# A mixture-of-experts tail with its second layer transposed and its combine weights spread over partitions by a transfer

## The chip, the cores and the metric

One core of one Trainium2 chip (trn2). The metric is the device time of one execution in microseconds (us), median of several; lower is better.

## What is computed

Two transformer layers on x of B = 2 batches, S = 512 tokens, D = 128 features, all in fp32. The parts of the last stage are what the change touches:

```python
# after two attentions: x = layernorm(x + attn_out)
gp = softmax(xt @ w_group + b_group); g_idx = argmax(gp); g_prob = max(gp)
ep_sel = softmax(xt @ w_expert[g_idx] + b_expert[g_idx]); e_idx = argmax(ep_sel); e_prob = max(ep_sel)
combine = one_hot(g_idx * 2 + e_idx, 8) * (g_prob * e_prob)          # (tokens, 8)
h = relu(einsum('td,edf->etf', xt, w1) + b1)                          # 8 experts, 256 hidden
y = einsum('etf,efd->etd', h, w2) + b2
out = layernorm(xt + einsum('te,etd->td', combine, y)) + x1           # x1 is the layer's input
```

Ahead of it stand a ternary-weight FFN with 8-bit activations and two 16-head attentions (the first one causal, with an image key). Every expert is computed for every token.

## The kernel before, in words

The kernel is written engine by engine with semaphores. `MERGE` (line 46) is a string in which each letter takes the next step of one chain of work, and `program_order()` (line 58) turns it into one list of steps. Every engine walks the same list and issues its part of each step, in that order, so the string alone sets the order on all queues: TensorE (PE), VectorE (DVE), ScalarE (ACT), GpSimd (POOL) and SyncE (SP, whose queue issues nearly all DMAs). Steps are named with an instance: 0 and 1 are the two batches in the first attention, 2 and 3 in the second; in the expert stage 0 and 1 are the batches. Below, y1.3 is step `y` of batch 1, expert 3.

PSUM is cut into places: `misc`, `pv`, `s0`, `s1` of one bank (512 fp32 columns) and `t0`, `t1` of two. `place_jobs()` (line 137) counts the jobs of each place in the order of the list; PE waits before it writes a place until all earlier jobs of that place have been freed, and readers wait for the fill count.

The order of the stages: the FFN of batch 0 (steps ffn_in to x1t), the small products `images` (PE lines 1156 to 1174, for which DVE and ACT take the results at lines 905 and 719), q, k and v of batch 0, three-part bf16 splits of q and k on DVE (lines 950 to 963), which SP writes to DRAM and loads back stacked (line 501), then the `scores` of all instances (PE line 1253, row maxima on DVE lines 985 and 989), beside them `attend` (PE line 1276, exp on ACT line 770) and `values` (PE line 1294). Scores of batch 0 wait for the stacked q and k.

The expert stage, per batch, with the lines of each step:

- `presum` and `sum` (PE lines 1321 to 1331) form x + attention in rows, `centre` and `spread` normalise it on DVE (lines 817 to 833) with a power on POOL (line 639), `x3t` transposes it into X3T (PE line 1337, ACT line 776).
- `router` (PE line 1345), `routed` and `route` (DVE lines 1038 to 1075) give `comb`, a column of 8 weights for each token; `combine` transposes it to combT, 8 partitions of 512 tokens (PE line 1352, ACT line 779); `bias2` multiplies it with b2 (four matmuls, PE line 1359) and `acc0` adds X3 into acc (DVE line 1080).
- For each of the 8 experts `hidden` makes two 128x512 halves of the first layer in s0 and s1 (PE line 1369, two matmuls of 512 columns), `relu` is taken on DVE for s0 (line 1084) and on ACT for s1 (line 756) into `hid`, which has two buffers; `y` (PE line 1377) uses `hid` as the weights and W2 as the streamed operand, in 4 token tiles by 2 halves, 8 matmuls of 128 columns, into `misc`; `add` (DVE line 1093) adds each of the 4 tiles, times the token's combine weight, to acc.
- At the end `centre` and `spread` with i = 1 normalise acc and add x1, and SP stores it (line 550).

A 4-byte matmul shows as two MATMUL records, so `y` is 16 records and `hidden` is 4. The expert steps of batch 0 start while the attention of instance 3 is still running; those after it follow on PE almost back to back.

## Time and profile before

| | |
|---|---|
| median of 3 runs | 357.32 us (356.76 to 358.71) |
| the profiled execution's own time | 352.93 us |
| its span | 351.1 us |
| busy: PE, PE weight loads, DVE, ACT, POOL | 293.8, 149.9, 258.8, 168.8, 29.3 us |
| mean granted TensorE clock | 0.96 |
| DMA | 22.83 MB |

The span is the time from the first to the last instruction of the profile; the execution's own time has 1.8 us more around it. Busy times overlap. A matmul's end is modelled, so distances between starts are the better measure on PE. A row of the views below says engine, line, output<-input, shape and count, then busy time, mean, and what ended the idle time before.

### The profile page before, as it was taken

Reading aid. Unit: us, or ns where it says so; the run is one execution under the profiler, and the core shown is the slowest. Engines: PE = TensorE matmul, PEld = TensorE weight load, DVE = VectorE, ACT = ScalarE, POOL = GpSimd, SP = SyncE. Lnnn points to the kernel's source line nnn. Section 1 sums busy time; section 2 is a strip of 40 time slices with the busy share of each in tenths; the row PEclk is TensorE's granted clock in tenths of the full one; section 3 lists DMA queues with packets and bytes.
Section 4 is the critical chain, followed back from the end, with each engine's and each line's share of the span. In section 5 each row is a group of like instructions: output and inputs, shape, how many; then the busy total and the mean of one; then the engine's idle time right before and its main releaser. Section 6 shows DMA issues by size and latency. Waiting matters only on the chain.

```text
span 351.1 us, 5408 instructions
## 1 busy us (share of the span) xinstructions
PE 293.8 (84%) x1862; PEld 149.9 (43%) x1888; DVE 258.8 (74%) x764; ACT 168.8 (48%) x246; POOL 29.3 (8%) x58
## 2 busy tenths in 40 slices
PE   0286945988889999789999999999899999899981
PEld 0134531345445554244342332334334457656760
DVE  6888687999767788979999788777813128558445
ACT  1864360055555686166286676674767621221110
POOL 3075000000000000600000000003000001001001
PEclk9999686599999999999999999999999999999997
DMA  6892157214620027800037500260000000001001
GB/s 191 177 194 57 27 158 175 58 34 141 166 57 3 2 74 200 156 7 2 2 86 189 130 1 0 56 187 2 0 2 2 0 2 1 2 0 30 0 2 31
DMA packets 14959, 22.83 MB, mean 65 GB/s; under 512 B 2190, under 2 KB 12306, under 8 KB 14164
## 3 DMA queue, kind: packets, MB, share of 16 engines
q1 hardware_dynamic: 14644, 22.21, 25.7%
q0 software_dynamic: 288, 0.28, 0.7%
q8 instruction: 15, 0.25, 0.3%
q14 instruction: 12, 0.10, 0.1%
HBM read 13.99 MB, written 4.72 MB: 53 GB/s over the span
## 4 chain that ended last, share of the span: by engine, by line
PE 43%; DVE 22%; issue 14%; DMA 10%; ACT 6%; SPq 2%; POOL 1%; POOLq 0%; another core or an unknown queue 0%; DVEq 0%; ACTq 0%
PE ps_pv L1294 10%; DVE mx L989 9%; PE ps_t L1276 7%; PE ps_s L1253 6%; DMA Qs<-nmT 6%; PE ps_s L1369 5%; PE ps_misc L1377 4%; ACT probs L770 3%; DVE shared L985 2%; DMA shared<-in_L_ffn_w_down 2%; DVE probs L919 1%; DVE shared L833 1%; DVE q L922 1%; DVE mx L985 1%; DMA Ks<-parts_k 1%
## 5 line engine op out<-in xcount | busy, mean ns | idle before, releaser
L770 ACT ACTIVATE probs<-ps_t 128x1024 f32<-128x1024 f32 (+2 forms) x128 | 105.6, 862 | 61.8 <-PE ps_t L1279 26.4
L989 DVE TENSOR_REDUCE mx<-ps_s 128x1 f32<-128x512 f32 x126 | 80.8, 685 | 13.7 <-PE ps_s L1253 12.4
L1253 PE MATMUL ps_s<-Ks,Qs 128*128 128x512 bf16 (+3 forms) x220 | 70.6, 347 | 11.0 <-DVE mx L985 2.8
L1276 PE MATMUL ps_t<-Qs,Ks 128*128 128x512 bf16 (+3 forms) x245 | 65.4, 338 | 6.2 <-DMA Qs<-nmT 3.8
L1294 PE MATMUL ps_pv<-probs,Vs 128*32 128x512 f32 (+3 forms) x512 | 55.5, 522 | 0.3 <-ACT probs L770 0.2
L985 DVE CUSTOM_DVE_ANT_0 shared<-ps_s,shared 128x128 bf16<-128x128 f32 (+3 forms) x106 | 45.6, 459 | 10.4 <-PE ps_s L1253 9.5
L1253 PEld LDWEIGHTS ps_s<-Ks,Qs 128*128 128x128 bf16 x232 | 21.7, 98 | 57.9 <-DVE mx L989 26.8
L1093 DVE SCALAR_TENSOR_TENSOR shared<-ps_misc,comb,shared 128x128 f32<-128x128 f32 x64 | 18.0, 343 | 31.1 <-PE ps_misc L1377 31.1
L1276 PEld LDWEIGHTS ps_t<-Qs,Ks 128*128 128x128 bf16 x256 | 23.5, 98 | 32.4 <-issue 10.7
L1377 PE MATMUL ps_misc<-Ks,shared 128*128 128x128 f32 x256 | 31.6, 277 | 4.2 <-DVE shared L1093 1.4
L1377 PEld LDWEIGHTS ps_misc<-Ks,shared 128*128 128x128 f32 x256 | 30.5, 192 | 9.6 <-issue 8.2
L1369 PE MATMUL ps_s<-Qf,Ks 128*128 128x512 f32 x64 | 30.3, 596 | 0.0
L756 ACT ACTIVATE shared<-ps_s,cols 128x512 f32<-128x512 f32 x16 | 11.0, 686 | 36.7 <-PE ps_s L1369 36.7
L1279 PE MATMUL ps_t<-causal_k,identb 128*128 128x128 bf16 x128 | 24.5, 219 | 0.3 <-issue 0.2
L1294 PEld LDWEIGHTS ps_pv<-probs,Vs 128*32 128x32 f32 x512 | 11.4, 108 | 21.2 <-issue 20.0
L639 POOL TENSOR_TENSOR shared<-shared,halves 128x4 f32<-128x4 f32 x4 | 4.1, 1036 | 193.7 <-DVE shared L823 193.7
L753 ACT ACTIVATE shared<-ps_pv 128x512 f32<-128x512 f32 x16 | 9.6, 597 | 12.1 <-PE ps_pv L1294 12.0
L1369 PEld LDWEIGHTS ps_s<-Qf,Ks 128*128 128x128 f32 x64 | 11.0, 191 | 9.5 <-issue 9.0
L1084 DVE TENSOR_SCALAR shared<-ps_s,cols 128x512 f32<-128x512 f32 x16 | 11.9, 744 | 3.4 <-PE ps_s L1369 3.4
L1279 PEld LDWEIGHTS ps_t<-causal_k,identb 128*128 128x128 bf16 x128 | 12.5, 98 | 3.2 <-issue 0.3
L985 DVE CUSTOM_DVE_ANT_0 shared<-ps_t,shared 128x512 bf16<-128x512 f32 (+1 forms) x22 | 13.0, 626 | 0.0
L633 POOL TENSOR_TENSOR Zimg<-Vimg,Pimg 128x288 f32<-128x288 f32 x4 | 2.7, 682 | 107.6 <-ACT Pimg L750 107.6
(244 smaller groups left out, 324.2 us busy)
## 6 DMA issues: line engine op xcount, KB each, us to landing
parts_q<-Qp SPq DMA_DIRECT2D x20, 128.0 KB, 1.9
Qs<-parts_q SPq DMA_DIRECT2D x24, 96.0 KB
Ks<-parts_k SPq DMA_DIRECT2D x24, 96.0 KB
Qs<-parts_q SPq DMA_DIRECT2D x12, 192.0 KB
Ks<-parts_k SPq DMA_DIRECT2D x12, 192.0 KB
Ks<-Qs SPq DMA_DIRECT2D x2, 1024.0 KB, 12.0
parts_k<-Kp SPq DMA_DIRECT2D x12, 128.0 KB, 1.8
Qs<-Qs SPq DMA_DIRECT2D x1, 1024.0 KB, 12.2
```

The lines of the kernel that those rows point to most:

```text
L756: act.activation(hid[:, i % 2, 1, :], ps[:, :], ACT.Relu, bias=cols17[:, 2 * i + 1:2 * i + 2])\
L770: act.activation(probs[:, half % 2, j, 0:w], ps[:, 0:w], ACT.Exp).then_inc(free[f"t{i % 2}"], 1)
L985: last = dve.tensor_tensor_reduce(out=added[:, n % 2, 0:w], in0=ps[:, 0:w], in1=causal_q[:, S - w:], scale=1.0, scalar=LEAST, op0=ALU.add, ...
L989: last = dve.tensor_reduce(mx[:, b, t, h:h + 1], ps[:, 0:w], AX, ALU.max)
L1084: dve.tensor_scalar(hid[:, i % 2, 0, :], ps[:, :], cols17[:, 2 * i:2 * i + 1], 0.0, ALU.add, ALU.max).then_inc(free["s0"], 1)
L1093: last = dve.scalar_tensor_tensor(out=acc[:, a, t, :], in0=ps[:, t * D:(t + 1) * D], scalar=comb[:, a, t, i // 2, i % 2:i % 2 + 1], in1=ac ...
L1253: mm = pe.matmul(ps[:, 0:w], Qs[:, b, h, t * P:(t + 1) * P], Ks[:, b, h, 0:w], start=True, stop=True)
L1276: mm = pe.matmul(ps[:, col:col + w], Ks[:, b, h, kb * P:(kb + 1) * P], Qs[:, b, h, S - w:S], start=True, stop=(a >= 2))
L1279: mm = pe.matmul(ps[:, col:col + P], identb[:, :], causal_k[:, :], start=False, stop=True)
L1294: mm = pe.matmul(ps[j * HC:(j + 1) * HC, S - w:S], Vs[:, b, kb, r * GROUP + j, :], probs[:, half % 2, j, col:col + w], start=(kb == 0), st ...
L1369: pe.matmul(ps[:, :], W1[:, i, h * P:(h + 1) * P], X3T[:, a, :], start=True, stop=True)\
L1377: mm = pe.matmul(ps[:, t * D:(t + 1) * D], hid[:, i % 2, h, t * P:(t + 1) * P], W2[:, i, h, :], start=(h == 0), stop=(h == FH - 1))
```

## The change

1. `y` takes W2 as weights and streams `hid`: two matmuls of 512 columns, out transposed (features on partitions, tokens along the row). For batch 0 each expert's result goes to `misc` and DVE adds it to accT; for batch 1 all 16 matmuls and `bias2` accumulate in `pv`, and DVE adds once, in two halves.
2. The combine weight now multiplies `hid` (new step `scale`, two 128x512 products on DVE for each expert). The weights must stand along the row on all 128 partitions: SP writes combT (16 KB) to DRAM, waits for it, and loads it back to combB with every partition reading the same rows, 512 KB for experts 0 and 1 and 1.5 MB for the other six, each with its own semaphore. combB lies in Qs.
3. `relu` of both halves is on ACT.
4. `bias2` is one matmul of 512 columns.
5. A new step `rows` turns accT back (4 transposes), and `centre` reads that from PSUM.
6. `MERGE` is another string, with other places for steps of every stage. Among them: `images` stands after k0 instead of ahead of the third `ffn_up` of batch 1; `x1` of batch 1 on DVE stands after 5 steps of scores instead of before the first; POOL's `stacks` of batch 0 stands ahead of `turn_weights`; `load_small` is earlier and `load_experts` 5 scores later.

The order of PE's steps in the last stage, before:

```
y0.1 values hidden0.2 turn_back hidden0.3 o_rows presum1 y0.2 sum1 hidden0.4 y0.3 hidden0.5 y0.4 hidden0.6
x3t1 y0.5 hidden0.7 router1 y0.6 hidden1.0 combine1 y0.7 hidden1.1 bias2_1 y1.0 hidden1.2 y1.1 hidden1.3 y1.2
hidden1.4 y1.3 hidden1.5 y1.4 hidden1.6 y1.5 hidden1.7 y1.6 y1.7
```

and after:

```
y0.1 values hidden0.2 turn_back hidden0.3 o_rows presum1 y0.2 sum1 hidden0.4 y0.3 hidden0.5 x3t1 y0.4
hidden0.6 y0.5 hidden0.7 router1 y0.6 combine1 hidden1.0 bias2_1 y0.7 hidden1.1 rows0 y1.0 hidden1.2 y1.1
hidden1.3 y1.2 hidden1.4 y1.3 hidden1.5 y1.4 hidden1.6 y1.5 hidden1.7 y1.6 y1.7 rows1
```

The diff, cut to its core:

```diff
+        accT = XT
+        combB = Qs[:, :, :, :].rearrange("p b h s -> p b (h s)").bitcast(fp32)\
+            .rearrange("p b (e s) -> p b e s", e=EXPERTS)
...
+                if step == "combine":
+
+                    sp.wait_ge(free["misc"], filled("misc", "combine", a))
+                    sp.dma_start(comb_dram[a], combT[:, a, :]).then_inc(comb_stored[a], 16)
+                    sp.wait_ge(comb_stored[a], 16)
+                    sp.wait_ge(full["t1"], filled("t1", "weights", 2 + a, UNITS - 1))
+                    for g, (lo, hi) in enumerate(((0, 2), (2, EXPERTS))):
+                        sp.dma_start(combB[:, a, lo:hi, :].rearrange("p e s -> p (e s)"),
+                                     drows(comb_dram[a][lo:hi, :], P, (hi - lo) * S)).then_inc(comb_spread[a][g], 16)
...
                 if step == "relu":
-                    ps = take("s1", "hidden", a, i)
-                    act.activation(hid[:, i % 2, 1, :], ps[:, :], ACT.Relu, bias=cols17[:, 2 * i + 1:2 * i + 2])\
-                       .then_inc(free["s1"], 1)
+                    for h in range(FH):
+                        ps = take(f"s{h}", "hidden", a, i)
+                        act.activation(hid[:, i % 2, h, :], ps[:, :], ACT.Relu,
+                                       bias=cols17[:, 2 * i + h:2 * i + h + 1]).then_inc(free[f"s{h}"], 1)
...
+                    dve.wait_ge(free["misc"], filled("misc", "x3t", a))
+                    dve.tensor_tensor(accT[:, a, :], ps[:, :], X3T[:, a, :], ALU.add).then_inc(free["misc"], 1)
+                if step == "scale":
+                    dve.wait_ge(comb_spread[a][i // 2 > 0], 16)
+                    for h in range(FH):
+                        dve.wait_ge(free[f"s{h}"], filled(f"s{h}", "hidden", a, i))
+                        last = dve.tensor_tensor(hid[:, i % 2, h, :], hid[:, i % 2, h, :], combB[:, a, i, :], ALU.mult)
+                    last.then_inc(scaled, 1)
+                if step == "add" and a == 0:
...
-                    for t in range(NT):
-                        last = dve.scalar_tensor_tensor(
-                            out=acc[:, a, t, :], in0=ps[:, t * D:(t + 1) * D],
-                            scalar=comb[:, a, t, i // 2, i % 2:i % 2 + 1], in1=acc[:, a, t, :],
-                            op0=ALU.mult, op1=ALU.add)
-                    last.then_inc(free["misc"], 1)
+                    dve.tensor_tensor(accT[:, a, :], ps[:, :], accT[:, a, :], ALU.add).then_inc(free["misc"], 1)
+                if step == "add" and a == 1:
+                    ps = take("pv", "outputs", a)
+                    dve.wait_ge(free["misc"], filled("misc", "x3t", a))
+                    half = S // 2
+                    for n in range(2):
+                        last = dve.tensor_tensor(accT[:, a, n * half:(n + 1) * half], ps[:, n * half:(n + 1) * half],
+                                                 X3T[:, a, n * half:(n + 1) * half], ALU.add).then_inc(summed[a], 1)
...
+                    ps = put("misc", "bias2", a) if a == 0 else put("pv", "outputs", a)
+                    mm = pe.matmul(ps[:, :], B2[:, :], combT[:, a, :], start=True, stop=(a == 0))
...
                 if step == "y":
+                    pe.wait_ge(scaled, NTH["scale", a, i])
+                    ps = put("misc", "y", a, i) if a == 0 else place["pv"]
                     for h in range(FH):
+                        mm = pe.matmul(ps[:, :], W2[:, i, h, :], hid[:, i % 2, h, :],
+                                       start=(a == 0 and h == 0), stop=(h == FH - 1 and (a == 0 or i == EXPERTS - 1)))
...
+                if step == "rows":
+                    if a == 0:
+                        pe.wait_ge(free["misc"], filled("misc", "y", a, EXPERTS - 1))
+                    ps = put("misc", "rows", a)
                     for t in range(NT):
-                        for h in range(FH):
-                            mm = pe.matmul(ps[:, t * D:(t + 1) * D], hid[:, i % 2, h, t * P:(t + 1) * P],
-                                           W2[:, i, h, :], start=(h == 0), stop=(h == FH - 1))
+                        if a == 1:
+                            pe.wait_ge(summed[a], t // 2 + 1)
+                        mm = pe.transpose(ps[:, t * P:(t + 1) * P], accT[:, a, t * P:(t + 1) * P], ident[:, :])
                     mm.then_inc(full["misc"], 1)
```

## Rows read from the trace of the kernel before

**Rows 1.** Windows of 20 us: busy time of PE, PEld, DVE, ACT, POOL; clock, DMA, GB/s
```profile
60.00:80.00 20.00, 17.30 (x75) 8.01 (x74) 19.48 (x89) 5.89 (x9) 0.68 (x1) 0.74 0.22 53
...
300.00:320.00 20.00, 17.18 (x104) 12.39 (x102) 11.79 (x49) 3.95 (x7) 1.04 (x1) 1.00 0.00 1
```

**Rows 2.** Groups by line and shape, 280 us to the end
```profile
L1377 PE MATMUL ps_misc<-Ks,shared 128*128 128x128 f32 x224 | 27.7, 277 | 4.2 <-DVE shared L1093 1.4 <-DVE shared L1080 0.9 <-ACT Qf L776 0.8
L1377 PEld LDWEIGHTS ps_misc<-Ks,shared 128*128 128x128 f32 x224 | 26.6, 192 | 9.3 <-issue 8.2 <-DVE shared L1084 1.0
...
L1093 DVE SCALAR_TENSOR_TENSOR shared<-ps_misc,comb,shared 128x128 f32<-128x128 f32 x57 | 16.1, 343 | 22.8 <-PE ps_misc L1377 22.8
```

**Rows 3.** The chain that ended last: start us, length us, what
```profile
290.99 1.72 PE ps_s L1369 x4
292.70 1.78 PE ps_misc L1377 x16
...
300.00 0.45 PE ps_misc L1337 x4
...
304.96 0.81 PE ps_misc L1345 x8
...
314.83 1.10 PE ps_misc L1359 x8
```

**Rows 4.** PE's waits from 290 us on: total us, times, longest
```profile
PE ps_misc L1377 <- DVE shared L1093: 1.4, 1, 1.4
PE ps_misc L1377 <- DVE shared L1080: 0.9, 1, 0.9
PE ps_misc L1377 <- ACT Qf L776: 0.8, 1, 0.8
```

**Rows 5.** Groups by line and shape, whole span
```profile
L770 ACT ACTIVATE probs<-ps_t 128x1024 f32<-128x1024 f32 x64 | 62.5, 1021 | 27.1 <-PE ps_t L1276 24.0 <-remote 1.7 <-PE ps_pv L1294 1.1
...
L756 ACT ACTIVATE shared<-ps_s,cols 128x512 f32<-128x512 f32 x16 | 11.0, 686 | 36.7 <-PE ps_s L1369 36.7
...
L1080 DVE TENSOR_TENSOR shared<-ps_misc,shared 128x512 f32<-128x512 f32 x2 | 1.4, 690 | 8.4 <-PE ps_misc L1359 8.4
```

**Rows 6.** Timeline of the expert stage: start us, length us, engine, line
```profile
308.33 0.18 DVE L1074 TENSOR_TENSOR comb<-rg,comb 128x16 f32<-128x16 f32 x1
...
341.21 2.02 PE L1377 MATMUL ps_misc<-Ks,shared 128*128 128x128 f32 x16 [1.38 <-DVE shared L1093]
343.34 1.12 DVE L1093 SCALAR_TENSOR_TENSOR shared<-ps_misc,comb,shared 128x128 f32<-128x128 f32 x4 [2.28 <-PE ps_misc L1377]
```

**Rows 7.** DMA issues: out<-in, count, KB each, median us from issue to landing
```profile
parts_q<-Qp SPq DMA_DIRECT2D x20, 128.0 KB, 1.9
...
Ks<-Qs SPq DMA_DIRECT2D x2, 1024.0 KB, 12.0
...
Ks<-in_L_ffn_w SPq DMA_DIRECT2D x1, 1024.0 KB, 5.8
```

**Rows 8.** A 2 us window while the two 1 MB expert weights load
```profile
229.00:231.00 2.00, 2.00 (x14) 0.57 (x13) 1.68 (x3) 1.48 (x2) 0.00 (x0) 1.00 1.08 344
```

**Rows 9.** Timeline from the small products to the first scores
```profile
34.42 0.38 PE L1159 MATMUL ps_s<-WsqT,condT 128*128 128x128 f32 x2
...
35.23 1.12 DVE L946 SCALAR_TENSOR_TENSOR X<-ps_pv,q,X 128x128 f32<-128x128 f32 x4
...
38.12 1.63 PE L1173 MATMUL ps_s<-WinT,WcpT 128*128 128x384 f32 x2
...
45.60 0.69 DVE L953 TENSOR_TENSOR qres<-Qf,Qp 128x512 f32<-128x512 f32 x1
...
49.18 0.75 DVE L936 TENSOR_SCALAR shared<-probs 128x512 bf16<-128x512 f32 x2
...
55.66 0.33 PE L1253 MATMUL ps_s<-Ks,Qs 128*128 128x128 bf16 x2 [2.13 <-issue]
```

**Rows 10.** The window in which exp, the first experts and the last attention overlap
```profile
248.00:278.00 30.00, 29.02 (x181) 13.18 (x185) 9.99 (x35) 22.30 (x28) 0.00 (x0) 1.00 0.00 1
```

More of the change, by code:

```diff
@@ L98, in program_order @@
         "y": both("y", EXPERTS),
-        "z": both("add", EXPERTS),
+        "z": each("add", 0, EXPERTS) + [("add", 1, EXPERTS - 1)],
+        "&": both("scale", EXPERTS),
     }
@@ L110, in program_order @@
         chains["ns"[b]] = [(n, b, 0) for n in ("presum", "sum", "x3t", "router", "combine", "bias2")]
-        chains["QR"[b]] = [(n, b, 0) for n in ("centre", "spread", "routed", "route", "acc0")]
-        chains["op"[b]] = [("centre", b, 1), ("spread", b, 1), ("out", b, 0)]
+        chains["QR"[b]] = [(n, b, 0) for n in ("centre", "spread", "routed", "route")] + [("acc0", 0, 0)] * (b == 0)
+        chains["op"[b]] = [("rows", b, 0), ("centre", b, 1), ("spread", b, 1), ("out", b, 0)]
     taken = {name: iter(steps) for name, steps in chains.items()}
@@ L164, in place_jobs @@
         if step in ("x1t", "q", "k", "v", "o_rows",
-                    "x3t", "router", "combine", "bias2"):
+                    "x3t", "router", "combine", "rows") or step == "bias2" and a == 0:
             add("misc", step, a)
+        if step == "bias2" and a == 1:
+            add("pv", "outputs", a)
         if step == "presum":
@@ L187, in place_jobs @@
             waiting -= 1
-            add("misc", "y", a, i)
+            if a == 0:
+                add("misc", "y", a, i)
     return places
@@ L233, in two_layers @@
                        for n, count in (("q", 2 * PARTS - 1), ("k", PARTS))] for a in range(INST)]
+        comb_dram = [nc.dram_tensor(f"parts_comb{b}", (EXPERTS, S), fp32, kind="Internal").ap() for b in range(B)]
         ident = sb("ident", [P, P])
@@ L428, in two_layers @@
         rstd_ready = [sem(f"rstd_ready{n}") for n in range(2 * B)]
-        gained = [sem(f"gained{b}") for b in range(B)]
         x3_ready = [sem(f"x3_ready{b}") for b in range(B)]
@@ L432, in two_layers @@
         comb_ready = sem("comb_ready")
+        comb_stored = [sem(f"comb_stored{b}") for b in range(B)]
+        comb_spread = [[sem(f"comb_spread{b}_{g}") for g in range(2)] for b in range(B)]
+        scaled, summed = sem("scaled"), [sem(f"summed{b}") for b in range(B)]
         out_ready, stored = [sem(f"out_ready{b}") for b in range(B)], sem("stored")
@@ L1079, in _ @@
                     ps = take("misc", "bias2", a)
-                    dve.tensor_tensor(acc[:, a, :, :], ps[:, :].rearrange("p (t d) -> p t d", d=D),
-                                      X3[:, a, :, :], ALU.add).then_inc(free["misc"], 1)
-                if step == "relu":
-                    ps = take("s0", "hidden", a, i)
-                    dve.tensor_scalar(hid[:, i % 2, 0, :], ps[:, :], cols17[:, 2 * i:2 * i + 1], 0.0,
-                                      ALU.add, ALU.max).then_inc(free["s0"], 1)
-                if step == "add":
+                    dve.wait_ge(free["misc"], filled("misc", "x3t", a))
[7 more added lines that the diff above has]
+                if step == "add" and a == 0:
                     if i == 0:
@@ L1091, in _ @@
                     ps = take("misc", "y", a, i)
[L1092 to L1097 removed]
+                    dve.tensor_tensor(accT[:, a, :], ps[:, :], accT[:, a, :], ALU.add).then_inc(free["misc"], 1)
[6 more added lines that the diff above has]
+                                                 X3T[:, a, n * half:(n + 1) * half], ALU.add).then_inc(summed[a], 1)
                 if step == "centre" and i == 1:
[L1099 to L1100 removed]
+                    ps = take("misc", "rows", a)[:, :].rearrange("p (t d) -> p t d", d=D)
+                    centre(2 + a, ps, acc[:, a, :, :], 2).then_inc(free["misc"], 1)
                 if step == "spread" and i == 1:
[L1102 removed]
+                    dve.wait_ge(free["misc"], filled("misc", "rows", a))
                     dve.wait_ge(residual_ready[a], 1)
@@ L1356, in _ @@
                     pe.wait_ge(free["misc"], filled("misc", "combine", a))
-                    ps = put("misc", "bias2", a)
-                    for t in range(NT):
-                        mm = pe.matmul(ps[:, t * D:(t + 1) * D], combT[:, a, t * P:(t + 1) * P], B2[:, :],
-                                       start=True, stop=True)
-                    mm.then_inc(full["misc"], 1)
+                    ps = put("misc", "bias2", a) if a == 0 else put("pv", "outputs", a)
+                    mm = pe.matmul(ps[:, :], B2[:, :], combT[:, a, :], start=True, stop=(a == 0))
+                    if a == 0:
+                        mm.then_inc(full["misc"], 1)
                 if step == "hidden":
```

26 lines of the change are left out of this document (13 added, 13 removed).

## The prediction, made before the change was run

> **What bounds the kernel now.** I read the windows first. From 60 to 80 us DVE is the full engine, with 19.48 of 20 us busy; from 300 to 320 us it is PE, with 17.18 of 20 against 11.79 for DVE and 3.95 for ACT [rows 1]. The change rewrites the expert stage, so its price is read on PE. The groups by shape say that y's matmuls are spaced by the work and not by waits: 4.2 us of waiting against 27.7 us busy in 14 steps [rows 2]. The chain gives the distances: two hidden matmuls of 512 columns take 1.72 us, and a y step of eight of 128 columns takes 1.78 us [rows 3]. Both stream 1024 columns. The waits name what stops PE there, each time because `misc` is still held: 1.4 us for the last adds, 0.9 us for acc0, 0.8 us for the copy of X3T [rows 4].
>
> **y.** The new y streams 2 times 512 columns, the shape of hidden, so I take 1.72 for 1.78 us: 0.06 us for each of 16, 1.0 us in all. The twelve weight loads that go were under the matmuls already. They are 26.6 us of busy time in 14 steps, 1.9 us a step [rows 2]; beside matmuls of 1.71 us nose to tail they would make a step 3.6 us long, and it is 1.78 us.
>
> The Trainium skill ("TensorE: Matmul & The Clock Gate", "The mechanism") says that a weight load overlaps a running matmul only when the row group differs. These all use the whole array, so by that rule the loads lie on the path and the change saves far more. By it the sum would be that of rival 5, by the trace it is the 1.0 us above. The trace disagrees with the rule, with its 1.78 us.
>
> **DVE and ACT.** The four adds of 343 ns [rows 2] and DVE's half of relu go; two products of 128x512 come, at 690 ns like acc0 [rows 5], 1.38 us, and for batch 0 one add of 0.69 us. ACT takes two relus of 686 ns [rows 5], 1.37 us. PE needs 3.44 us for a hidden and a y, so both are hidden wherever PE has a full pair to do. They would show where y follows its hidden closely. The last one does: hidden1.7 ends, y1.6 runs 1.72 us, then y1.7 needs relu and product, 0.7 + 0.7 us. 0.3 us of cover are left.
>
> **The expert stage on PE.** Let S be the end of sum1 (290.99) and R the end of router1 (305.77) [rows 3]. Before, R is S+14.8.
> - S to R holds the same steps. x3t1 is earlier, and the copy of X3T stands behind relu0.5 on ACT, so y0.4 waits 1.0 us where y0.5 waited 0.8 [rows 4]; three y and their restarts give some 0.6 back. R is S+14.4.
> - Before, after R: y0.6, hidden1.0, combine1, y0.7, hidden1.1, bias2, y1.0 and on, with PE's end at 341.21+2.02 = 343.23 [rows 6], R+37.5.
> - After: y0.6 waits 0.4 us for `routed` and ends at R+2.2. Now combine1 is next. It needs comb, which stood at 308.33+0.18 [rows 6], R+2.75, and `misc`, which add0.6 frees; that add is behind route on DVE, so R+3.45. PE idles 1.3 us. This is new: hidden1.0 covered that stretch. combine1 ends at R+4.0 and its copy on ACT, priced like a relu of 0.69 us [rows 5], at R+4.7.
> - PE goes on: hidden1.0 R+5.7, bias2 (0.9 us as one matmul, 1.10 as four [rows 3]) R+6.6, y0.7 R+8.3, hidden1.1 R+10.0, rows0 (0.45 like x3t [rows 3]) R+10.5. y1.0 could start there.
> - The spread: SP writes 16 KB, which lands after 1.9 us like the writes of parts_q [rows 7], and issues the loads at R+6.7. The 512 KB lie between 1.9 us for 128 KB and 5.8 us for 1 MB [rows 7], so 3.4 us, landing at R+10.1; the products end at R+11.5. y1.0 waits 1.0 us.
> - The other 1.5 MB: the expert weights move at 344 GB/s [rows 8], so 2 MB take 6.1 us and about 2 us of start and landing: R+15. By the row of 5.8 us for 1 MB it would be R+17. y1.2 would start at 11.5+4x1.72 = R+18.4 and needs it by R+17.0. No wait, with little or no margin at the dear end.
> - From y1.0 there are 14 pieces of 1.72 us: PE ends at R+35.6 instead of R+37.5. The waits of 0.9 and 1.4 us are gone, since y of batch 1 no longer shares `misc`.
>
> Sum: y0.0 to y0.2 -0.2, S to R -0.4, after R -1.9: -2.5 us.
>
> **The end.** Before, the last adds take 1.12 us after PE [rows 6]. Now two half adds of some 0.4 us (a 512-column one is 0.69 [rows 5]), with the first transposes under the second, then the last two transposes and their way out, 1.3 us. +0.2 us. centre and spread keep their price, as does the store.
>
> **The spread of batch 0.** The same sum as above gives 1.9+3.4+1.4 = 6.7 us and some issue time from the copy of combine0 to the end of the products. Between combine0 and y0.0 stand ten attend steps, whose exps of 1.02 us each [rows 5] alone are 10.2 us. So it is hidden. Without that cover PE would wait at y0.0 for what is late, with attention queued behind it, and exp on ACT after that.
>
> **relu on ACT beside exp.** From 248 to 278 us ACT is busy 22.3 of 30 us and PE 29.0 [rows 10]. Two more relus of 0.69 us come in. Free if they fall in ACT's gaps, 1.4 us if PE waits for each. I take 0.5, since PE is the fuller engine.
>
> **The new order.** `images` leaves the path of batch 0. It holds PE from 34.42 to 39.75 [rows 9] while x1t0 could start at 36.35, when the sums of x1 are done [rows 9]. With it gone DVE does ffn_up1.2 and 1.3 from 37.7 us and starts the parts of q near 41.6 instead of 45.60 [rows 9], 4 us earlier; so k's parts and both loads. But `images` then stands between k0 and batch 1's r2t on PE (41.8 to 47.3) and its copy is ahead of r2t's work on ACT, so DVE reaches r2t1.0 at 48.6 instead of 49.18 [rows 9]. The down products end near 53, and scores start there instead of at 55.66 [rows 9]: -2.6 us. x1 of batch 1, 1.12 us [rows 9], now falls into the full DVE stretch and was in the gap before it. Net -1.5 us, which I carry to the end, since DVE and then PE are full in between. Bounds: 0 (lost at a later join) and -4 (q's lead all used). Moves of single values, turns and sends by a few steps in the middle have no price that I can read: none, between -2 and +2.
>
> **POOL and SP.** POOL's earlier memsets fall into a wait. load_small goes onto POOL's queue, load_experts onto SP's, both far ahead of need. SP's wait for the stored 16 KB has only `out` behind it; no max_rows step follows combine.
>
> **Sum.** -2.5 + 0.2 + 0.5 - 1.5 = -3.3 us on an execution of 352.93 us: 349.6. That execution is 4.4 us under the median of the runs shown, so I move the median by as much: 357.3 - 3.3 = 354.0 us.
>
> **Rivals.**
> 1. *The spread arrives late (slower).* Every partition reads the same 16 KB of DRAM, which no transfer here does at this size. Against it: 344 GB/s [rows 8] with rows shorter than these. For it: a 1 MB copy from 64 partitions to 64 others took 12.0 us [rows 7]. It decides once the 1.5 MB land after R+17.0, 10.3 us after the issue; each us beyond is one on PE. At 12 us a MB they land at R+31, and 512 KB at R+13: y1.2 starts at R+32.3 instead of 18.4, +14 us, 368 us. At 160 GB/s they take 14 us, +4 us, no gain: 358 us.
> 2. *The order's gain is lost.* The first stage's 1.5 us go at a later join, and relu beside exp costs its 1.4: -2.5+0.2+1.4 = -0.9, 356.4 us. For it: ACT and PE are both near full in [rows 10].
> 3. *The order costs.* The middle loses 2 to 4 us at the long waits for the row of maxima behind the stacks: 357 to 360 us.
> 4. *q's lead is used in full.* -4 instead of -1.5: 351.5 us.
> 5. *Weight loads are on the path.* Then 12 of 16 loads of each y, 1.4 us, go: 16x1.4 = 23 us, 331 us. The 1.78 us of [rows 3] speak against it. (The rule of the Trainium skill quoted above would give this.)
>
> That the change doesn't do what it says: the stream of columns is the same, so the transposition itself gives 1 us. It is in the forecast.
>
> **How the numbers follow.** A measurement of this kernel can tell about 0.5%, 1.8 us, from no change. Forecast (352.3 to 355.5) 42%, rival 4 13%, rival 5 1%; rival 2 23%; rival 3 9%, rival 1 12%, of which a third ends within 1.8 us. Faster: 42+13+1 = 56%. Same: rival 2, part of 1 and 3, 27%. Slower: 17%. The range reaches down over rival 4 with -2 us of the middle, 349.5, and up over rival 3, 360.
>
> **What would show it.** y as 4 records in 1.72 us; first scores near 53 us; PE idle 1.3 us ahead of combine1 and 1.0 us ahead of y1.0; no wait of PE for `misc` in batch 1; scale1.2 not waiting for the transfer beyond R+17; PE's end at S+50. Wrong if y is much shorter than 1.72 us, if DVE waits for combB for more than a us or two, or if the first scores start at 55 us or later.

## The result and the profile after

| | before | after |
|---|---|---|
| median of 20 runs each | 356.64 us (352.44 to 361.86) | 360.96 us (355.31 to 370.22) |
| the profiled execution's span | 351.1 us | 355.5 us |
| busy: PE, PE weight loads, DVE, ACT | 293.8, 149.9, 258.8, 168.8 us | 293.7, 131.2, 256.3, 180.7 us |

The change makes the kernel slower: ratio after to before 1.0156, 95% interval [1.0108, 1.0205]. (Ratios leave disturbed, slower runs out and medians here are of all runs, so the two can differ by up to 0.8 per cent; where they disagree, neither is taken to settle a step smaller than that.) The forecast was 354.0 us; the time also lies above its range, which ended at 360.

**The expert stage is what I said.** Two parts of the chain of after, start us, length us, what:

```profile
297.11 1.72 PE ps_s L1393 x4
298.83 1.72 PE ps_misc L1399 x4
...
310.73 0.81 PE ps_misc L1370 x8
...
314.19 0.69 DVE XT L1115
314.88 0.14 issue
315.02 0.61 PE ps_misc L1377 x4
315.65 0.59 ACT X L800
316.26 1.45 DMA parts_comb<-X
317.73 4.08 DMA Qs<-parts_comb
```

A y step is 4 records in 1.72 us instead of 16 in 1.78 [rows 3]. S, the end of sum1, is 297.11 here and 290.99 before. R, the end of router1, is 311.54: S+14.4, as worked out. PE's waits from 296 us on:

```profile
PE ps_misc L1377 <- DVE XT L1115: 1.2, 1, 1.2
PE ps_misc L1399 <- ACT Qf L797: 0.9, 1, 0.9
PE ps_pv L1399 <- DVE shared L1107: 0.7, 1, 0.7
```

1.2 us ahead of combine1 (1.3 forecast) and 0.7 us ahead of y1.0, which waits for the spread weights (1.0 forecast). The row of y1.0:

```profile
323.19 1.98 PE L1399 MATMUL ps_pv<-shared,Ks 128*128 128x512 f32 x4 [0.73 <-DVE shared L1107]
```

That is R+11.65 against R+11.5. The spread's 512 KB took 4.08 us (3.4 forecast), and nothing waits for its 1.5 MB. From S to the end of the span it is 355.5 - 297.11 = 58.4 us; before it was 351.1 - 290.99 = 60.1. So this stage gives 1.7 us, where I had 2.1 (0.4 up to R and 1.9 behind it, less 0.2 at the end).

**The start is what I said, too.** The first scores:

```profile
53.35 0.33 PE L1278 MATMUL ps_s<-Ks,Qs 128*128 128x128 bf16 x2 [2.26 <-issue]
```

53.35 instead of 55.66 us [rows 9]. By the second row of score maxima (PE's max_rows, 91.97 us after and 93.14 before) a lead of 1.2 us is left, where I had said 1.5 net. But S is 6.1 us later. Between these two the profile loses 7.3 us, 7.2 of them up to the last row of maxima at 258 us, ahead of the first expert step, in a stretch where the change almost only moves steps.

PE's max_rows steps from there on, us:

| | 0.1 | 1.0 | 1.1 | 2.0 | 2.1 | 3.0 | 3.1 | S |
|---|---|---|---|---|---|---|---|---|
| before | 93.14 | 116.89 | 139.55 | 170.87 | 194.13 | 220.18 | 252.10 | 290.99 |
| after | 91.97 | 119.61 | 142.43 | 172.81 | 198.55 | 225.35 | 258.13 | 297.11 |
| difference | -1.2 | +2.7 | +2.9 | +1.9 | +4.4 | +5.2 | +6.0 | +6.1 |

The largest step, 3.9 us, is the first. (The new order has max_rows2.0 three scores earlier in the list, so the gain of 1.0 us there is only its place, and comes back in the next column.)

**Where it goes.** Every half of an instance has a row of score maxima, which PE transposes (max_rows), ACT copies and SP sends into the stacked q as two transfers of 8 KB. The first attend step of that half waits for it. All of PE's waits for this transfer, in the trace of after and then of before (us in total, times, longest):

```profile
PE ps_t L1301 <- DMA Qs<-nmT: 4.9, 2, 2.6
PE ps_t L1304 <- DMA Qs<-nmT: 3.5, 1, 3.5
```

```profile
PE ps_t L1276 <- DMA Qs<-nmT: 3.8, 3, 2.6
```

8.4 us against 3.8. The one of 3.5 us in the timeline of PE, after:

```profile
101.29 0.22 PE L1304 MATMUL ps_t<-causal_k,identb 128*128 128x128 bf16 x1 [3.47 <-DMA Qs<-nmT]
```

and the step that waits for the same transfer before:

```profile
98.49 1.71 PE L1294 MATMUL ps_pv<-probs,Vs 128*32 128x512 f32 x16
100.36 0.22 PE L1253 MATMUL ps_s<-Ks,Qs 128*128 128x128 bf16 x1 [0.16 <-issue]
101.56 0.39 PE L1276 MATMUL ps_t<-Qs,Ks 128*128 128x512 bf16 x1 [0.98 <-DMA Qs<-nmT]
```

In both, the row is there at about the same time, 101.3 and 101.6 us. Before, PE did scores and values until 1.0 us ahead of that. After, it has none left in front of the waiting step from 97.8 us on: the new string puts 10 scores and 1 values step between max_rows and the first attend that needs its row, where the old one puts 13 and 2. At instance 1 it is 9 instead of 12 scores (2 values in both), at the second half of instance 2 it is 7 scores and 1 values step instead of 8 and 2. PE issues in order, so scores that stand behind the waiting attend can't fill the gap, and DVE, the full engine of this stretch, runs dry beside it. Windows of 2 us over the wait, after and then before (busy PE, PEld, DVE, ACT, POOL; clock, DMA, GB/s):

```profile
96.00:98.00 2.00, 1.73 (x12) 0.35 (x10) 1.53 (x7) 0.49 (x1) 0.00 (x0) 1.00 0.80 160
98.00:100.00 2.00, 0.00 (x0) 0.00 (x0) 0.16 (x2) 0.00 (x0) 0.00 (x0) 1.00 0.28 60
100.00:102.00 2.00, 0.71 (x9) 0.49 (x14) 0.12 (x1) 0.00 (x0) 0.00 (x0) 1.00 0.00 1
102.00:104.00 2.00, 2.00 (x11) 0.37 (x11) 0.87 (x5) 0.61 (x1) 0.00 (x0) 0.52 0.00 0
104.00:106.00 2.00, 2.00 (x15) 0.77 (x14) 1.56 (x7) 1.22 (x2) 0.00 (x0) 0.62 0.00 0
```

```profile
98.00:100.00 2.00, 2.00 (x19) 0.61 (x18) 1.77 (x9) 0.57 (x2) 0.00 (x0) 1.00 0.60 121
100.00:102.00 2.00, 0.86 (x8) 0.38 (x6) 0.98 (x5) 0.00 (x0) 0.00 (x0) 1.00 0.01 2
102.00:104.00 2.00, 2.00 (x27) 1.06 (x25) 0.91 (x4) 1.68 (x3) 0.00 (x0) 1.00 0.00 0
```

DVE does 0.16 and 0.12 of 2 us. And there is a second effect: behind PE's idle time the granted clock falls to 0.52 and 0.62, the lower of its two levels for most of 4 us, while before it stays at 1.00.

All that is reading. It says where the time is; whether the moved steps cause it, the runs had to say.

### The profile page after: what moved, and what is told of

Its sections match the earlier page's. It is cut to its first block, busy times and chain, and to the rows that moved or that the text cites. A ratio compares the mean times of both kernels' runs of the same rounds, so it can differ in the third digit from the quotient of the medians.

```text
span 355.5 us, 5002 instructions
## 1 busy us (share of the span) xinstructions
PE 293.7 (83%) x1665; PEld 131.2 (37%) x1692; DVE 256.3 (72%) x725; ACT 180.7 (51%) x262; POOL 28.6 (8%) x58
## 4 chain that ended last, share of the span: by engine, by line
PE 47%; DVE 20%; issue 13%; DMA 9%; ACT 8%; SPq 1%; POOL 1%; POOLq 0%; DVEq 0%; ACTq 0%
PE ps_pv L1319 12%; PE ps_s L1278 8%; DVE mx L1010 7%; PE ps_t L1301 7%; DMA Qs<-nmT 6%; PE ps_s L1393 4%; ACT probs L791 4%; PE ps_misc L1399 3%; DMA shared<-in_L_ffn_w_down 2%; DVE shared L1006 1%; PE ps_misc L1254 1%; PE ps_t L1304 1%; DMA Qs<-parts_comb 1%; DVE shared L854 1%; DVE mx L1006 1%
## 5 line engine op out<-in xcount | busy, mean ns | idle before, releaser
L1010 DVE TENSOR_REDUCE mx<-ps_s 128x1 f32<-128x512 f32 x128 | 81.7, 685 | 15.9 <-PE ps_s L1278 11.2
L1278 PE MATMUL ps_s<-Ks,Qs 128*128 128x512 bf16 (+3 forms) x221 | 71.5, 351 | 11.0 <-DVE mx L1006 3.7
L1006 DVE CUSTOM_DVE_ANT_0 shared<-ps_s,shared 128x256 bf16<-128x256 f32 (+3 forms) x109 | 47.7, 464 | 16.2 <-PE ps_s L1278 15.2
L1319 PE MATMUL ps_pv<-probs,Vs 128*32 128x512 f32 (+3 forms) x512 | 57.6, 530 | 1.4 <-issue 0.5
L1278 PEld LDWEIGHTS ps_s<-Ks,Qs 128*128 128x128 bf16 x237 | 22.3, 99 | 67.5 <-DVE mx L1010 31.3
L1107 DVE TENSOR_TENSOR shared<-shared,Qs 128x512 f32<-128x512 f32 x32 | 21.1, 687 | 20.2 <-ACT shared L777 18.7
L777 ACT ACTIVATE shared<-ps_s,cols 128x512 f32<-128x512 f32 x32 | 21.6, 686 | 27.4 <-PE ps_s L1393 27.4
L1399 PE MATMUL ps_misc<-shared,Ks 128*128 128x512 f32 x32 | 15.3, 600 | 1.3 <-ACT Qf L797 0.9
L1399 PE MATMUL ps_pv<-shared,Ks 128*128 128x512 f32 x32 | 15.0, 597 | 0.7 <-DVE shared L1107 0.7
L1115 DVE TENSOR_TENSOR XT<-ps_misc,XT 128x512 f32<-128x512 f32 x8 | 5.5, 689 | 14.0 <-PE ps_misc L1399 14.0
L1006 DVE CUSTOM_DVE_ANT_0 shared<-ps_t,shared 128x512 bf16<-128x512 f32 (+1 forms) x19 | 11.3, 624 | 0.8 <-remote 0.8
```

The lines of the kernel that those rows point to most:

```text
L777: act.activation(hid[:, i % 2, h, :], ps[:, :], ACT.Relu, bias=cols17[:, 2 * i + h:2 * i + h + 1]).then_inc(free[f"s{h}"], 1)
L1006: last = dve.tensor_tensor_reduce(out=added[:, n % 2, 0:w], in0=ps[:, 0:w], in1=causal_q[:, S - w:], scale=1.0, scalar=LEAST, op0=ALU.add, ...
L1010: last = dve.tensor_reduce(mx[:, b, t, h:h + 1], ps[:, 0:w], AX, ALU.max)
L1107: last = dve.tensor_tensor(hid[:, i % 2, h, :], hid[:, i % 2, h, :], combB[:, a, i, :], ALU.mult)
L1278: mm = pe.matmul(ps[:, 0:w], Qs[:, b, h, t * P:(t + 1) * P], Ks[:, b, h, 0:w], start=True, stop=True)
L1319: mm = pe.matmul(ps[j * HC:(j + 1) * HC, S - w:S], Vs[:, b, kb, r * GROUP + j, :], probs[:, half % 2, j, col:col + w], start=(kb == 0), st ...
```

## The experiments

The string was cut into five sections: *start* (up to the fifth scores step), *A* (to o_rows0), *B* (to max_rows2.0), *C* (to o_rows2), *D* (to hidden0.0). Behind them comes the expert stage. Each kernel has after's code or before's, and in each section the old order of steps or the new one. Medians are of all runs of a kernel; every ratio is to the kernel before, on the same chip.

**1. The expert code or the order ahead of it?** e1 has the new code and expert order, and the old order in all five sections. e2 is the mirror.

```diff
 e1: after, with
-start A B C D: new order
+start A B C D: order of before
 e2: before, with
-start A B C D: old order
+start A B C D: order of after
```

> The code of the changed kernel; the order of all steps ahead of the first expert step (hidden0.0) is that of the kernel before, the order from there on is the changed one. Theory O (the order ahead of the experts costs some 7 us, the new expert stage gives about 2): about 2 us faster than the kernel before, ratio 0.993 to 0.996, and the sum step of batch 1 ends near 291 us of the span as in the kernel before. Theory C (the new code costs it: relu beside exp, the transfers, the products): the ratio stays near 1.015 and the time is lost after 255 us.

> The mirror of it: the code of the kernel before, with the changed order ahead of hidden0.0 and the old one from there on. Theory O: 5 to 8 us slower than the kernel before, ratio 1.015 to 1.022. Theory C: within 0.5% of the kernel before.

| | median | ratio |
|---|---|---|
| e1_old_front | 355.96 us | 0.9919 [0.9851, 0.9988] |
| e2_new_front | 364.37 us | 1.0179 [1.0091, 1.0267] |

The new expert stage, alone, gains a little (0.9 us by the medians, and by the ratio's interval 0.1 to 1.5%); the new order, alone, costs as much as the whole change or more. The price is in the order.

**2. The start, and the router earlier.** e3 is e1 with the new *start*; e4 is e1 with router1 and routed/route of batch 1 moved ahead of y0.5, and combine1 ahead of y0.6.

```diff
 e4, TensorE's steps:
-y0.4 hidden0.6 y0.5 hidden0.7 router1 y0.6 combine1
+y0.4 hidden0.6 router1 y0.5 hidden0.7 combine1 y0.6
```

> As e1, but the order up to the fifth scores step is the changed one (images behind k0, x1 of batch 1 later), the old one between there and hidden0.0. If the 2.3 us by which the first scores came earlier are carried to the end, it is 1.2 us or more faster than e1 (ratio 0.990); if a later join swallows them, it is the same as e1 (0.995).

> As e1, with router1, routed and route ahead of y0.5, and combine1 ahead of y0.6. The wait ahead of combine1 (1.15 us) and the one ahead of y1.0 (0.73 us) go, and one of about 0.75 us for the copy of combT ahead of y0.6 comes. Expected 1.1 us faster than e1, ratio 0.990 to 0.992. If y1.0's wait stays, the transfer and not the place of the router holds it.

e3: 354.18 us, ratio 0.9956 [0.9909, 1.0002]. e4: 353.54 us, 0.9976 [0.9918, 1.0034]. Neither can be told from e1 by these intervals, nor can a small gain or cost be excluded. In e4's trace the waits ahead of combine1 and of y1.0 (1.2 and 1.1 us in e1's) are gone and one of 0.9 us for the copy of combT has come, as expected.

**3. Which section?** e5 to e8 are e1 with the new order in one section alone.

> e1 with the changed order in one stretch alone: from scores0.5 to o_rows0 (about 54 to 125 us). In the trace of the changed kernel that stretch is 4.9 us longer than before, 1.1 us of it x1 of batch 1; PE waits 3.5 us at once for the row of maxima behind the stack loads, where it waited 1.0 us. Theory F (the order is lost at the waits for the row of maxima, where the filling steps were taken earlier): 3 to 4 us slower than e1, ratio to the kernel before 1.000 to 1.004, with the 3.5 us wait in the profile. Theory G (a spread loss, each move a little, or the lead of the start that cannot be kept): under 1 us slower than e1.

> e1 with the changed order from o_rows0 to the first max_rows of instance 2 alone (125 to 171 us). Both traces need the same time for it within 0.7 us: same as e1, ratio 0.990 to 0.996, by either theory.

> e1 with the changed order from there to o_rows2 alone (171 to 237 us). The traces differ by 1.7 us over it and by 4.9 us at its worst place, where the changed kernel waits 2.3 us for the row of maxima of instance 2. Theory F: 2 to 3 us slower than e1, ratio near 0.999, with that wait in the profile. Theory G: under 1 us.

> e1 with the changed order from o_rows2 to hidden0.0 alone (237 to 256 us). The changed kernel lost 2.6 us here, 1.6 us of them in one wait of PE for a row maximum on DVE. If that is this order's own, 1.5 to 2.5 us slower than e1, ratio near 0.998; if it came from what was late before, the same as e1.

| new order in | median | ratio |
|---|---|---|
| A (e5) | 358.03 us | 1.0101 [1.0014, 1.0188] |
| B (e6) | 360.66 us | 1.0186 [1.0101, 1.0272] |
| C (e7) | 357.77 us | 0.9944 [0.9834, 1.0054] |
| D (e8) | 354.90 us | 1.0016 [0.9960, 1.0072] |

A and B cost, and each more than the 1.000 to 1.004 that I had expected for A. C stays open: its interval is the widest of the four, and its median is 1.0 us above that of before. I had expected nothing of B, a miss: I had looked at the wait near 100 us alone. B holds the second wait, with 9 scores of cover instead of 12. The longest waits for the row in e5 and e6:

```profile
PE ps_t L1304 <- DMA Qs<-nmT: 4.6, 1, 4.6
```

```profile
PE ps_t L1301 <- DMA Qs<-nmT: 5.7, 3, 3.9
```

**4. The cover alone.** Sections move many steps. e9 is after, whole, with three scores put back ahead of each of the two waiting attends; e10 is e1 with three scores taken away there. The values steps between go with them, so the cover isn't quite that of the other two kernels (see the table). e9's next attend of that instance, attend.17, moves by a step or two as well.

```diff
 e9 (from after), instance 0; the like at instance 1
-scores1.12 attend0.16 scores1.13 scores1.14 values0.5 scores1.15 attend0.17 keep0.1
+scores1.12 scores1.13 scores1.14 values0.5 scores1.15 attend0.16 keep0.1 scores1.16 attend0.17
 e10 (from e1), instances 0 and 1
-scores1.13 scores1.14 values0.4 values0.5 normalise0.0 scores1.15 scores1.16 attend0.16
+scores1.13 attend0.16 scores1.14 values0.4 values0.5 normalise0.0 scores1.15 scores1.16
-scores2.10 scores2.11 values1.5 scores2.12 scores2.13 attend1.16
+scores2.10 attend1.16 scores2.11 values1.5 scores2.12 scores2.13
```

> The changed kernel whole, with its own order, but the first attend steps of the second half of instances 0 and 1 moved back behind three more scores steps, so that 13 and 12 scores stand between the row of maxima and the step that needs its transfer, as in the kernel before (the changed kernel has 10 and 9). Theory F (the loss is the uncovered wait for the row and the TensorE clock that falls after it: 3.5 us of wait and 3.4 us at a clock near 0.55 in the changed kernel's trace at 98 to 106 us, and 2.3 us of wait in the second place): 3 to 5 us back of the changed kernel's 361, so 356 to 358, ratio to the kernel before 1.000 to 1.004, and the wait near 100 us down from 3.5 to 1.5 us or less. Rival (other moves of the string cost the time): ratio stays near 1.015, whatever the wait shows.

> The mirror: the new expert code with the order before ahead of the experts (355.96 us, ratio 0.992 in its own run), and only attend0.16 and attend1.16 moved three scores steps earlier, which leaves 10 and 9 scores to cover the transfer. Theory F: 3 to 5 us slower than that kernel, 359 to 361, ratio 1.000 to 1.008, a wait of 3 to 4.5 us near 100 us. Rival: one step moved at each of two places changes nothing that can be measured, ratio 0.99.

| | scores in the cover | values in it | median | ratio |
|---|---|---|---|---|
| after | 10, 9 | 1, 2 | 360.96 us | 1.0156 [1.0108, 1.0205] |
| e9_refill | 13, 12 | 2, 4 | 356.41 us | 1.0012 [0.9965, 1.0060] |
| e1_old_front | 13, 12 | 2, 2 | 355.96 us | 0.9919 [0.9851, 0.9988] |
| e10_thin | 10, 9 | 0, 1 | 364.17 us | 1.0264 [1.0212, 1.0317] |

Both directions: one attend moved over three scores and the values between them, at each of two places, gives 4.5 us back, and takes 8 us away (I had expected 3 to 5 us of each). So the uncovered waits at these two places cause most of the loss. They aren't shown to cause all of it. Against before measured beside it, the order costs after 5.2 us over e1 by the medians, of which e9 has back 4.7; by the ratios it is 2.4% and e9 has back 1.4%. And e12 below, with the order of before in A, B and C, the same number of scores in the cover and the router one y earlier, has a ratio of 0.9888 [0.9838, 0.9938] against e9's 1.0012 [0.9965, 1.0060]. What else in the new A to C costs up to that difference stays open.

PE's waits for the row in the two traces, up to 275 us:

```profile
PE ps_t L1301 <- DMA Qs<-nmT: 5.3, 3, 2.1
```

```profile
PE ps_t L1301 <- DMA Qs<-nmT: 8.5, 4, 3.9
```

The first is e9, the second e10; e1's were 3.7 us in total. So e10's waits were 4.8 us longer in these two profiles, and its median is 8 us longer. A single profile is a rough measure of the waits: e4, with the order of e1 up to the experts, waited 7.5 us in its profiled execution, and after itself 8.4, about as much as e10. e9's profile has 5.3 us of waits, 2.1 of them at the third place, which it leaves alone. What a wait can cost beyond its length is question 6.

**5. Why is the row late?** SP's timeline in after, the first and the last of the stack loads that it issues (18 in all, not twelve, as my expectations have it) and the row:

```profile
83.68 1.25 SPq L540 DMA_DIRECT2D Qs<-parts_q  x3
...
90.34 1.18 SPq L546 DMA_DIRECT2D Ks<-parts_k  x3
93.44 1.34 SPq L551 DMA_DIRECT2D Qs<-nmT  x2
```

The row is issued at 93.44 and used from 101.29 us. The loads' traffic goes on until about 99 us (DMA share 0.80, 0.28 and 0.00 in the windows above; by half microseconds it falls to 0.11 at 99.0). With nothing else in flight the same transfer is quick. SP's issue and PE's step in e1's trace, in the second half of instance 3:

```profile
253.80 1.39 SPq L551 DMA_DIRECT2D Qs<-nmT  x2
```

```profile
256.74 0.38 PE L1301 MATMUL ps_t<-Qs,Ks 128*128 128x512 bf16 x1 [0.55 <-DMA Qs<-nmT]
```

2.9 us against 7.9. e11 is after with the row issued by ACT, on a queue that nothing else uses then:

```diff
-sp.wait_ge(free["misc"], filled("misc", "max_rows", a, i))
 for n in range(2):
-    sp.dma_start(Qs[SHIFT + n:...], nmT[...]).then_inc(shifted[a][i], 16)
+    act.dma_start(Qs[SHIFT + n:...], nmT[...]).then_inc(shifted[a][i], 16)
```

> The changed kernel with its own order, but the two small transfers of each row of maxima are issued by ACT, right after it has copied the row, and not by SP behind the twelve loads of the stacked parts. If the row is late because it stands behind those loads in one queue (2.4 MB moving until 98 us, row landed at 101.3): it lands within 3 us of its issue, both long waits go, and ACT pays some 0.7 us for each issue, 16 of them, in a stretch where it has room: 353 to 357, ratio 0.99 to 1.00. If the row is late because all transfers share the engines whatever the queue: the landing stays near 101 us, the wait near 3.5 us, and the time is 361 or more.

363.55 us, ratio 1.0156 [1.0085, 1.0227]: no gain. The queue theory falls. ACT's timeline of e11, and the step that used the row:

```profile
95.17 1.29 ACTq L764 DMA_DIRECT2D Qs<-nmT  x2
```

```profile
103.11 0.61 PE L1300 MATMUL ps_t<-Qs,Ks 128*128 128x512 bf16 x1 [2.34 <-DMA Qs<-nmT]
```

7.9 us from issue to use, the same as on SP's queue. So the row isn't late because of the queue it stands in. In both traces it is used soon after the loads' traffic ends: the DMA share falls to about 0.1 at 99.0 us in after and at 101.0 in e11, and the row is used 2.3 and 2.1 us behind that. What is left are the DMA engines. The Trainium skill ("DMA: Bandwidth & Descriptors", "Queues, rings and completion order") says that both queues run on the same 16 engines, and that the write which signals a transfer's end lands only after every earlier write of that engine, whichever queue it came from. The 7.9 us on either queue agree; that this is the cause is argued, not shown. Choosing another issuer doesn't move the landing; putting more work in front of the wait covers it.

**6. Does the fallen clock cost?** Across the profiles the stretch from one row of maxima to the next is a good yardstick, since the same order of steps comes with the clock up and down. "Lowest clock" is that of the four 2 us windows behind the wait:

| stretch, order | kernel | wait | lowest clock | length |
|---|---|---|---|---|
| second wait, old B | before | 2.55 us | 1.00 | 31.3 us |
| | e8 | 2.49 | 0.50 | 32.9 |
| | e1 | 2.90 | 0.50 | 34.4 |
| third wait, new C | after | 2.29 | 1.00 | 26.8 |
| | e13 | 3.95 | 0.50 | 31.1 |
| first wait, order of e9 | e13 | 0.38 | 1.00 | 24.9 |
| | e9 | 1.92 | 0.55 | 28.0 |

At the same wait (before, e8) the lower clock goes with 1.6 us; at the other three the stretch grows by 1.6 to 2.7 us more than the wait. Three more profiles with the old B fit: e5 (wait 2.38 us, clock at 1.00) took 31.2 us for it, e4 (2.81, down to 0.50) 33.2 and e3 (3.08, down to 0.54) 33.4. Windows of e8 and then of before, at that place:

```profile
150.00:152.00 2.00, 1.26 (x13) 0.52 (x13) 0.35 (x1) 0.50 (x1) 0.00 (x0) 0.95 0.23 39
152.00:154.00 2.00, 2.00 (x11) 0.80 (x7) 1.04 (x2) 0.45 (x2) 0.00 (x0) 0.50 0.00 0
154.00:156.00 2.00, 1.90 (x14) 0.83 (x14) 1.11 (x2) 1.53 (x2) 0.00 (x0) 0.69 0.00 0
```

```profile
150.00:152.00 2.00, 1.68 (x15) 0.71 (x16) 0.69 (x1) 0.92 (x1) 0.00 (x0) 1.00 0.02 2
152.00:154.00 2.00, 1.86 (x19) 0.95 (x19) 1.84 (x3) 1.38 (x2) 0.00 (x0) 1.00 0.00 0
154.00:156.00 2.00, 1.86 (x12) 0.94 (x12) 1.99 (x4) 1.91 (x4) 0.00 (x0) 1.00 0.00 0
```

PE is full in both. At 0.50 it can't feed DVE, which does 2.15 us of work in the last two windows instead of 3.83. But this compares profiles, not kernels. e15, e16 and e18 are after with extra matmuls that keep PE busy through the waits; their result is overwritten:

```diff
 ps = put(f"t{i % 2}", "weights", a, i)
+for n in range(EXTRA.get((a, i), 0)):      # e15: (0,16): 16, (1,16): 12, (2,0): 10
+    pe.matmul(ps[:, 0:S], Ks[:, b, h, 0:P], Ks[:, b, h, :], start=True, stop=True)
 if i % (UNITS // 2) == 0:
     pe.wait_ge(shifted[a][i // (UNITS // 2)], 16 * 2)
```

e16 has 20, 20 and 18. In both the third block stands at attend2.0, a wrong place: the third late row belongs to attend2.16. e18 has it there, with 18, 18 and 13.

> The changed kernel with its own order; ahead of its three late waits for the row PE does 16, 12 and 10 extra matmuls of 128x512 bf16 (0.22 us each, 3.5, 2.6 and 2.2 us) into the place that the waiting step is about to fill and overwrites. They leave the wait's end where the transfer lands and only keep PE busy. If the clock that falls after the wait is a part of the loss (0.52 and 0.62 from 102 to 106 us in the changed kernel's trace, some 1.7 us): the clock stays at 1.00 behind the first wait, and 1.5 to 3 us come back, 358 to 359.5, ratio 1.006 to 1.011. If the waits alone make the loss, and the throttled stretch is hidden beside DVE, the full engine: no change from 361, ratio 1.014 to 1.018.

> e15 (the changed kernel with extra matmuls ahead of the three late waits for the row) with 20, 20 and 18 instead of 16, 12 and 10. e15's profile kept the clock at the first wait (segment from the row of maxima to the next one 26.1 us instead of 27.6) and lost it at the second, where its 12 extra matmuls ended 2.3 us before the row landed (34.2 us instead of 30.4). If the fallen clock is a part of the loss and busy PE keeps it: no window below 0.9 behind any of the three waits, the three segments near 26, 30.5 and 26.5 us, and 1.5 to 3 us less than the changed kernel, 358 to 359.5, ratio 1.005 to 1.011. If the waits alone make the loss: 361 to 362, since the extra matmuls that run past the landing cost up to 1 us at each place.

> e15 and e16 had their third block of extra matmuls at attend2.0, where the trace shows nothing late: the third late row is that of the second half of instance 2, and the step that waits is attend2.16. There the block (2.3 us in e15, 4.1 us in e16, at 181 us, with DVE idle beside it) was pure cost. Here the changed kernel has 18, 18 and 13 extra matmuls at attend0.16, attend1.16 and attend2.16. If the fallen clock is a part of the loss: clock at 1.00 behind all three, segments near 26.5, 31 and 26.5 us, 358.5 to 360, ratio 1.006 to 1.012. If the waits alone make the loss: 361 to 362, ratio 1.014 to 1.018, as e15, whatever the clock shows.

| | median | ratio | the three stretches | lowest clock behind each |
|---|---|---|---|---|
| after | 360.96 us | 1.0156 [1.0108, 1.0205] | 27.6, 30.4, 26.8 us | 0.50, 1.00, 1.00 |
| e15_warm | 361.59 us | 1.0157 [1.0113, 1.0201] | 26.1, 34.2, 25.5 | 1.00, 0.50, 1.00 |
| e16_warm2 | 363.48 us | 1.0205 [1.0143, 1.0266] | 27.0, 31.9, 26.4 | 1.00, 1.00, 1.00 |
| e18_warm3 | 357.19 us | 1.0147 [1.0071, 1.0223] | 26.6, 31.5, 27.1 | 1.00, 1.00, 1.00 |

The extra matmuls do hold the clock: windows of e18 over the first wait, where PE is full and DVE as empty as in after:

```profile
98.00:100.00 2.00, 2.00 (x11) 0.89 (x10) 0.00 (x0) 0.00 (x0) 0.00 (x0) 1.00 0.05 11
100.00:102.00 2.00, 2.00 (x19) 0.85 (x16) 0.49 (x3) 0.00 (x0) 0.00 (x0) 1.00 0.00 0
102.00:104.00 2.00, 2.00 (x23) 0.73 (x16) 1.61 (x8) 1.52 (x2) 0.00 (x0) 1.00 0.00 0
```

The clock stays at 1.00 and DVE does 1.61 us from 102 to 104 instead of after's 0.87. But the sum shows no gain that can be measured: e18's ratio is after's. Its median is 2.4 us above that of before, where after's is 4.3 above, and the interval holds both. The blocks themselves cost where they outlast the transfer: they ran 4.05, 4.05 and 2.97 us in e18, and after's waits were 3.5, 2.6 and 2.3. e18's own expectation asked for 1.006 to 1.012 if the clock had a share and for 1.014 to 1.018 if it had none; its interval of [1.0071, 1.0223] holds both. Whether the lower clock has a share in the median, besides its place in single profiles, stays open.

**7. More cover, and the third place.** e12 puts together what had not cost: new *start*, old A, B and C, new D, the router earlier. e13 is e9 with attend2.0 two scores later; e14 is e12 with 15, 15 and 9 scores ahead of attend0.16, attend1.16 and attend2.0 instead of 13, 12 and 7. e17 is e12 with 8, 10 and 8 extra matmuls at attend0.16, attend1.16 and attend2.0.

> New expert code; order: the new start, the order before through the middle, the new order of the stretch just ahead of the experts, and in the expert stage router1, routed and route one y earlier. Each of the three parts alone gave 353.5 to 354.9 in its own run. If they add: 352 to 353, ratio 0.985 to 0.990. If they do not (the start's lead goes at the first long wait): 354, ratio 0.992 to 0.996.

> e9 (the changed kernel with 13 and 12 scores restored at two waits, 356.41 us, ratio 1.001) and in addition attend2.0 moved behind two more scores, at the third place where the row lands late (PE waited 2.1 us there in e9's trace, 2.3 us in the changed kernel's, 0.3 us before). If the waits for the row, at all three places, are the whole loss: the third wait goes to 1 us or less, and 1 to 2 us more come back, 354.5 to 355.5, ratio 0.995 to 0.998. If something else of the string costs the rest: no step from e9, ratio 1.001.

> e12 (the fastest so far, 351.62 us, ratio 0.989) with two or three scores steps more of cover at each of the three places than the kernel before has: 15, 15 and 9 instead of 13, 12 and 7. e12's trace still waits 1.7, 1.3 and 1.4 us there. If cover pays for each wait to its end: the three waits near 0 and 2 to 3.5 us less, 348 to 350, ratio 0.979 to 0.984. If the clock made the loss steep and the waits left are too short to set it off, or ACT's exps that start later cost as much: within 1 us of e12, ratio 0.987 to 0.991.

> e12 (the fastest so far, 351.62 us, ratio 0.989, waits of 1.7, 1.3 and 1.4 us with the clock at 1.00 behind each in its one profile) with 8, 10 and 8 extra matmuls ahead of the three waits. If the runs of e12 above its fastest lose the clock behind a wait now and then: 0.5 to 1 us less, ratio 0.984 to 0.988. If its waits are too short for that: no change, ratio 0.987 to 0.991.

| | median | ratio |
|---|---|---|
| e12_best | 351.62 us | 0.9888 [0.9838, 0.9938] |
| e13_refill3 | 357.31 us | 1.0028 [0.9980, 1.0075] |
| e14_fat | 352.40 us | 0.9852 [0.9789, 0.9916] |
| e17_best_warm | 353.15 us | 0.9905 [0.9858, 0.9952] |

e12 is faster than both kernels, 5.2 us under the median of before measured beside it. e13 changed nothing, as it had to: attend2.0 was not the late one. Its trace has a wait of 3.95 us at attend2.16, untouched, with the clock at 0.50 behind it. e14 took the waits for the row down to 1.6 us from e12's 4.3 and is not measurably faster; in its trace PE's waits for ACT's exps are longer instead, 1.8 us where e12's has 0.6:

```profile
PE ps_t L1301 <- ACT probs L791: 1.8, 4, 0.7
PE ps_t L1301 <- DMA Qs<-nmT: 1.6, 2, 1.2
```

No gain beyond the old cover could be measured by this means. e17 says the same of the clock in the fast version: none fell behind its waits in e12's profile, and there was nothing to hold.

## Why the prediction was wrong

- **y, 1.72 for 1.78 us; R at S+14.4; combine1's new wait; y1.0 at R+11.5:** right within 0.15 us each. The 16 weight loads of a y had been hidden, as their 1.9 us inside 1.78 said. The Trainium skill ("TensorE: Matmul & The Clock Gate", "The mechanism", the bullet on LDWEIGHTS) lets a load overlap only where the row group differs; by that rule, and with the trace's own load times, the twelve that go would have saved an estimated 1.4 us a step. The step lost 0.06: the trace disagrees, before and after. So rival 5 did not come.
- **The spread:** 512 KB landed in 4.08 us instead of 3.4, 1.5 MB in time. Rival 1 did not come.
- **The expert stage:** 1.7 us from S to the end instead of 2.1. e1's ratio of 0.9919 [0.9851, 0.9988] is the code with the new order of the last stage alone: a gain of 0.4 to 5.3 us, which bears out the sign and can't tell 1.7 from 2.1. From the last row of maxima to S, where relu of batch 0 stands beside exp, the two traces take 38.9 and 39.0 us; I had said 0.5 us for relu less 0.2 for y.
- **The new order's start:** first scores at 53.35, near 53 as said; a lead of 1.2 us at 93 us, 1.5 said.
- **The step that failed** is the last term of "the new order": "Moves of single values, turns and sends by a few steps in the middle have no price that I can read: none, between -2 and +2". In the profile it was +7.3 us, and e2's median was 7.5 us above before's. I had not counted what stands between each row of maxima and the attend that waits for it, though both orders were there to be counted, and before's trace showed two of these waits (0.98 and 2.55 us) with nothing left to cover them. Three scores less at each, of 0.28 to 0.69 us on DVE in that trace, could have been priced at 1 to 2 us a wait.
- **Rival 3** named this mechanism and this place, with 2 to 4 us and 9%. It happened, at about twice the price. (Its range of 357 to 360 us is also not 354.0 plus 2 to 4; it fits only if the start's 1.5 us are lost as well, which it doesn't say.) That the measured 360.96 lies only 1 us above the stated range is luck: the range's upper end was put over this rival, while the term itself stood at none. The price lacked the count at all three places, and the clock: in some executions it falls behind the wait, and the stretch takes 1.6 to 2.7 us more.

## What to carry to other kernels

When a list of steps is reordered, find first the waits that already show in the trace, and count for each how much work of the full engine stands between the event that starts the transfer and the step that waits for it, in the old list and in the new. An in-order engine can't use what stands behind the wait, so moving a waiting step ahead of three pieces of work can cost more than rewriting a whole stage gains. Time an order separately from the code that came with it: here the two parts had opposite signs.
